# One Trainium2 core, two self attentions: shifts added to the scores by products with ones, and unread products on TensorE

## The chip, the cores and the metric

The kernel runs on one core of one Trainium2 chip. The metric is the device time of one execution in microseconds (us), the median of several runs. The core's engines are TensorE (PE: matmuls, with its weight loads as PEld), VectorE (DVE), ScalarE (ACT), GpSimd (POOL) and SyncE (SP, which here issues DMAs).

## What is computed

A two-layer block on a stream `x` of 32 batches, 64 tokens each, width 128. Each layer has a cross attention over 1601 context rows, a self attention and a feed-forward part. The change is in the two self attentions, one in each layer (16 heads of width 8). Cut to what matters, the first is:

```python
q = _apply_rope((x @ wq).reshape(B, T, H, D), cos, sin)
k = _apply_rope((x @ w_down @ wk_up).reshape(B, T, H, D), cos, sin)
v = (x @ w_down @ wv_up).reshape(B, T, H, D)
scores = jnp.einsum('bqhd,bkhd->bhqk', q, k) / sqrt(D)
scores = jnp.where(allowed, scores, finfo.min)      # pages of 32 tokens
attn = jax.nn.softmax(scores, axis=-1)              # subtracts the row's maximum
out = jnp.einsum('bhqk,bkhd->bqhd', attn, v) @ wo
```

The second has plain projections with biases, and its mask lets a query and a key meet if either is among the 16 most important tokens of its batch.

## The kernel before

The kernel is one program in which each engine follows its own list, and semaphores join them. The stages follow each other: cross attention with the first feed-forward part, self attention SA0, the routed experts, cross attention XA1, self attention SA1, the tree feed-forward part. `self_attention` is called twice, for SA0 and SA1, with the same code. Its order of work is written out by hand, once for each engine.

Work goes in 16 steps, `p` = 0 to 15, of two batches (`u` = 0, 1) each. All 16 heads of both batches go through together. A step has these parts:

- GpSimd (`pool_queries`, L1290) writes the step's queries into `QW`, spread out so that one product serves several heads. For `p` of 4 and more it waits until the scores of step `p - 4` are done.
- TensorE, values (`pe_values`, L1165): one float32 product, two passes in the trace, into a bank of PSUM. VectorE moves it to `VS` with the bias (L1255).
- TensorE, maxima (`pe_maxima`, L1177): 16 products give scores with queries on partitions, two banks. VectorE takes the row maxima (`dve_maxima`, L1263) and writes minus the maximum as two bf16 parts into `MH` (`dve_shift`, L1273 and L1275).
- TensorE, shift products (`pe_shift_rows`, L1190): 16 products turn these columns into rows, two banks, of which two partitions each are used. ScalarE copies three of the four pieces (L1240) and VectorE one (`dve_shift_rows`, L1280) into partitions 32, 33, 96 and 97 of `QW`, next to the queries. The keys `KSA` hold ones there, so the scores come out with the shift in them.
- TensorE, scores (`pe_scores`, L1204): 16 products of 128 columns, with keys on partitions, in four parts of the array (`tile_position`). ScalarE takes the exponential of 128 x 1024 (`act_exp`, L1233).
- TensorE, weighted values (`pe_product`, L1219): 32 float32 products, 64 passes in the trace. ScalarE copies the result to `ABO` (`act_output`, L1245).

In the loop TensorE's order is: scores of `p`, weighted values of `p - 1`, values of `p + 1`, maxima of `p + 3`, shift products of `p + 2`. Ahead of the loop stand values 0, maxima 0 and 1, shift products 0, maxima 2 and shift products 1; I call this and the first steps the opening. The four banks of PSUM from number 4 on go round among values (V), maxima (M) and shift products (R), by the lists `first` and `later`; a job waits until the one four places ahead of it is emptied.

Ahead of SA0 stands the rotary stage (its products L1584 and L1585, VectorE's L1591 to L1600), ahead of SA1 the stage that finds the important tokens. `attention_out` (L1391 and on) follows each.

Of the kernel before, what the change touches and what calls it, by code (L numbers as in the profile page):

```python
# [26 lines left out]
CH = 512  # L27
# [188 lines left out]
def bass_perceiver_kernel(nc, xT, ctxT, wpack, bpack, experts, picks, trees, outT):  # L216
# [3 lines left out]
    with ctx:  # L220
# [37 lines left out]
        MH = sb("MH", [128, 2, 16, 2], BF16)  # L258
        epst = sb("epst", [128, 1], F32)
# [3 lines left out]
        DEC = sb("DEC", [128, 2, CH], BF16)  # L263
# [24 lines left out]


# [822 lines left out]
        def self_attention(role, eng, att, q_stacked, k_stacked, src, banks_ready, between=None):  # L1112


            pairs, kk, rows = B // 2, att.values_k, HALF + 1
            past = 1 if att is SA1 else 0
# [12 lines left out]
            later = [job for p in range(pairs) for job in  # L1129
                     (("V", p + 1, 0), ("M", p + 3, 0), ("M", p + 3, 1), ("R", p + 2, 0), ("R", p + 2, 1))]  # L1130
            for job in first + later:
                if job[1] < pairs:
                    owner.append(job)
                    filled_at[job] = len(owner)
                    by_job = {"act": 2} if job[0] == "R" and job[2] == 0 else emptied_by[job[0]]
# [32 lines left out]
            def pe_maxima(p):  # L1168
                eng.wait_ge(qbuilt, 2 * before + 2 * p + 2)
                if p == pairs // 2:  # L1170
                    eng.wait_ge(*k_stacked[1])
                for h in range(2):
                    bank_free(("M", p, h))
                for u in range(2):
                    for g in range(4):
                        for h in range(2):
                            mm = nc.tensor.matmul(work(("M", p, h))[:, (u * 4 + g) * S:(u * 4 + g + 1) * S],  # L1177
                                                  queries(p, u)[half[h], g * 128:(g + 1) * 128],
                                                  KSA[half[h], g, tokens(p, u)], start=True, stop=True,
                                                  tile_position=(64 * h, 0))  # L1180
                mm.then_inc(filled, 2)

            def pe_shift_rows(p):
                eng.wait_ge(negm, before + p + 1)
                for u in range(2):
                    bank_free(("R", p, u))
                    for g in range(4):
                        for h in range(2):
                            row = 32 + 64 * h
                            mm = nc.tensor.matmul(work(("R", p, u))[row:row + 2, g * 128:(g + 1) * 128],  # L1190
                                                  MH[:, p % 2, h * 8 + u * 4 + g, :], wb("ident16"),
                                                  start=True, stop=True, tile_position=(0, row))
                    mm.then_inc(filled, 1)

            def pe_scores(p):
                for u in range(2):
                    for by in emptied_at[("R", p, u)]:
                        eng.wait_ge(*emptied(("R", p, u), by))
                if before + p:
                    eng.wait_ge(exps, before + p)  # L1200
                for g in range(4):
                    for u in range(2):
                        for h in range(2):
                            mm = nc.tensor.matmul(  # L1204
                                ps[64 * u:64 * u + 64, h, g * 128:(g + 1) * 128], KSA[half[h], g, tokens(p, u)],
                                queries(p, u)[half[h], g * 128:(g + 1) * 128],
                                start=True, stop=True, skip_group_check=True, tile_position=(64 * h, 64 * u))
                mm.then_inc(scores, 1)
# [58 lines left out]
            def dve_shift(p):  # L1267
                for h in range(2):
                    eng.wait_ge(*emptied(("M", p, h), "dve"))
                if p >= 2:  # L1270
                    eng.wait_ge(*filled_with(("R", p - 2, 1)))
# [3 lines left out]
                nc.vector.scalar_tensor_tensor(MH[:, p % 2, :, 1], top, -1.0, MH[:, p % 2, :, 0],  # L1275
                                               ALU.mult, ALU.subtract).then_inc(negm, 1)
# [19 lines left out]
            if role == "pe":  # L1296
                eng.wait_ge(sem("value_pads"), 1)
                eng.wait_ge(*banks_ready)
                pe_values(0)
                eng.wait_ge(sem("ones_set"), 3)  # L1300
# [3 lines left out]
                pe_maxima(1)  # L1304
                pe_shift_rows(0)
# [24 lines left out]
            if role == "dve":  # L1330
                eng.wait_ge(*banks_ready)
                nc.vector.memset(ps[:, 2:4, :].rearrange("p a c -> p (a c)"), 0.0).then_inc(ready, 1)
# [5 lines left out]
                dve_shift_rows(0)  # L1338
                dve_maxima(2)
                dve_shift(2)  # L1340
                dve_shift_rows(1)
                for p in range(pairs):
# [5 lines left out]
                    if p + 2 < pairs:  # L1348
                        dve_shift_rows(p + 2)
# [885 lines left out]
        def program(role, eng):  # L2235
# [8 lines left out]
            if role == "dve":  # L2244
                nc.vector.memset(epst[:, :], EPS).then_inc(sem("eps_set"), 1)
                nc.vector.memset(HM[:, :], 0.0).then_inc(sem("half_zero"), 1)
                nc.vector.memset(VS[:, :, :].rearrange("p u (g i e) -> p (u g) i e", g=8, i=3)[:, :, 1, :], 0.0
# [340 lines left out]
```

## Time and profile before

| what | value |
|---|---|
| median of 3 runs | 1888.97 us (1885.73 to 1890.61) |
| the profiled execution | 1887.62 us, span 1885.8 us |
| TensorE busy | 1739.7 us, 92% of the span, 29724 matmul passes |
| VectorE, ScalarE, GpSimd busy | 1401.4, 1244.4, 581.2 us |
| mean granted TensorE clock | 0.959 |
| SA0 on TensorE | from 653.55 to about 719 us |
| SA1 on TensorE | from 1664.34 to about 1738 us |

The span is the time from the first to the last instruction on the core. Busy is the time in which an engine executes an instruction; TensorE's is modelled from the starts of pipelined matmuls, so starts are more exact than lengths. The granted clock is a share of full speed: 1.0 is 2.4 GHz and 0.5 is 1.2 GHz. The two attentions are about 140 of the 1886 us.

### The profile page before, as it was taken

To read this page: it belongs to the slowest core of one execution; us is meant where nothing else is said; L and a number is where in the kernel's file an instruction comes from. 1 tells how busy PE (TensorE), PEld (TensorE's weight loads), DVE (VectorE), ACT (ScalarE), POOL (GpSimd) and SP (SyncE) were. 2 spreads that over 40 slices of the span, in tenths; PEclk is the share of its full clock that TensorE was granted. 3 is DMA by queue.
4 is the path that set the end of the run, shared out by engine and by line. 5 is a ranking of instruction groups with operands and counts; after the bars stand their busy time and mean duration, and the time that the engine had idled before them with its cause. 6 is when DMAs were issued, how large, how long until landed. Compare 5 with 4: busy or idle time off the path is not lost. (4 is left out here: it accounts for less than half of the span.)

```text
span 1885.8 us, 68279 instructions
## 1 busy us (share of the span) xinstructions
PE 1739.7 (92%) x29724; PEld 1096.8 (58%) x29724; DVE 1401.4 (74%) x2431; ACT 1244.4 (66%) x2177; POOL 581.2 (31%) x463
## 2 busy tenths in 40 slices
PE   7899999999989778799889999999999999866998
PEld 5577777777765456344446666656666665535443
DVE  2577777777752785777789889888988997366565
ACT  3377777777754284224368888888888888367343
POOL 4223222322230350566522232222222220043465
PEclk8799999999999888999989999999999999879999
DMA  4355555555510211465565556555555652030111
GB/s 160 95 133 141 144 145 149 138 143 146 135 31 0 45 27 36 124 157 141 148 110 101 107 97 104 95 107 102 101 102 101 103 100 29 2 71 4 34 40 39
DMA packets 69149, 178.42 MB, mean 95 GB/s; under 512 B 20900, under 2 KB 25124, under 8 KB 68468
## 3 DMA queue, kind: packets, MB, share of 16 engines
q1 hardware_dynamic: 67076, 171.49, 41.4%
q8 instruction: 236, 3.87, 0.9%
q10 hardware_dynamic: 1776, 2.57, 0.7%
q14 instruction: 61, 0.50, 0.1%
HBM read 84.45 MB, written 1.32 MB: 45 GB/s over the span
## 5 line engine op out<-in xcount | busy, mean ns | idle before, releaser
L749 ACT ACTIVATE Pb<-ps 128x512 f32<-128x512 f32 (+1 forms) x832 | 451.9, 597 | 51.4 <-PE ps L693 32.6
L716 PE MATMUL ps<-Pb,V 128*17 128x64 f32 (+1 forms) x13312 | 380.5, 248 | 0.7 <-ACT Pb L749 0.7
L828 DVE TENSOR_REDUCE MX<-ps 128x2 f32<-128x804 f32 (+1 forms) x384 | 363.8, 983 | 21.3 <-PE ps L657 19.9
L716 PEld LDWEIGHTS ps<-Pb,V 128*17 128x17 f32 (+1 forms) x13312 | 250.4, 97 | 87.1 <-issue 43.6
L830 DVE TENSOR_REDUCE MX<-ps 128x1 f32<-128x402 f32 (+1 forms) x512 | 265.9, 569 | 29.8 <-PE ps L661 23.8
L872 POOL TENSOR_TENSOR ABO<-CT 128x1601 bf16<-128x1601 f32 x43 | 123.0, 2863 | 528.6 <-DMA CT<-ctxT 528.6
L752 ACT ACTIVATE Pb<-ps 128x1024 f32<-128x1024 f32 (+1 forms) x224 | 204.6, 959 | 42.6 <-PE ps L697 40.0
L657 PE MATMUL ps<-KST,QW 50*128 50x402 bf16 (+1 forms) x1024 | 176.0, 340 | 13.2 <-DVE C L814 4.5
L693 PE MATMUL ps<-QW,KST 50*128 50x128 bf16 (+1 forms) x3328 | 165.4, 219 | 5.1 <-ACT Pb L749 2.4
L775 ACT ACTIVATE V<-ps 128x512 f32<-128x512 f32 (+1 forms) x256 | 129.5, 521 | 42.4 <-PE ps L597 40.8
L661 PE MATMUL ps<-KST,QW 96*128 96x402 bf16 (+1 forms) x512 | 148.9, 340 | 5.8 <-DVE C L814 0.5
L693 PEld LDWEIGHTS ps<-QW,KST 50*128 50x128 bf16 (+1 forms) x3328 | 104.5, 96 | 73.5 <-ACT Pb L749 44.1
L1779 PE MATMUL ps<-ABO,CT 128*128 128x512 bf16 x362 | 115.2, 384 | 14.0 <-DVE ABO L1841 9.6
L597 PE MATMUL ps<-WS,ABO 128*128 128x128 bf16 x819 | 128.1, 219 | 0.0
L697 PE MATMUL ps<-QW,KST 98*128 98x128 bf16 (+1 forms) x1664 | 124.7, 219 | 2.3 <-ACT Pb L752 1.2
L697 PEld LDWEIGHTS ps<-QW,KST 98*128 98x128 bf16 (+1 forms) x1664 | 108.8, 99 | 16.6 <-ACT Pb L752 1.7
L597 PE MATMUL ps<-WS,CT 128*128 128x128 bf16 (+1 forms) x1118 | 111.2, 220 | 4.3 <-ACT V L775 1.2
L814 DVE SCALAR_TENSOR_TENSOR HL<-ps,W,HL 128x402 bf16<-128x402 f32 x124 | 74.7, 632 | 54.0 <-ACT HL L762 51.5
L814 DVE SCALAR_TENSOR_TENSOR C<-ps,W,C 128x402 bf16<-128x402 f32 (+1 forms) x128 | 77.0, 632 | 44.7 <-ACT C L762 41.8
L1831 ACT ACTIVATE Pb<-ps 128x512 f32<-128x512 f32 x68 | 40.6, 597 | 105.4 <-PE ps L1779 101.1
L657 PEld LDWEIGHTS ps<-KST,QW 50*128 50x128 bf16 x1024 | 51.5, 93 | 87.9 <-issue 43.3
L597 PEld LDWEIGHTS ps<-WS,CT 128*128 128x128 bf16 (+1 forms) x1118 | 87.4, 100 | 24.4 <-issue 12.3
(278 smaller groups left out, 3179.9 us busy)
## 6 DMA issues: line engine op xcount, KB each, us to landing
CT<-ctxT SPq DMA_DIRECT2D x43, 800.5 KB, 4.7
KST<-HL SPq DMA_DIRECT2D x320, 100.1 KB, 3.0
KST<-C SPq DMA_DIRECT2D x320, 100.1 KB, 3.0
Pb<-routed SPq DMA_DIRECT2D x44, 256.0 KB, 4.0
ABO<-ctxT SPq DMA_DIRECT2D x10, 800.5 KB, 5.6
T<-ctxT SPq DMA_DIRECT2D x10, 800.5 KB, 4.4
KST<-HL SPq DMA_DIRECT2D x128, 50.0 KB, 2.7
KST<-C SPq DMA_DIRECT2D x128, 50.0 KB, 2.7
```

The costliest lines, as they stand in the source:

```text
L597: mm = nc.tensor.matmul(work(job)[0:n, i * D:(i + 1) * D], still[:, k0:k0 + n], WS[:, 1, wp, :], start=(k == 0), stop=(k == 2))
L657: mm = nc.tensor.matmul(work(job)[:, h, 0:n], QW[half[h], b % 3, g * 128:(g + 1) * 128], KST[half[h], b % 3, g, c0:c0 + n], start=True, st ...
L661: mm = nc.tensor.matmul(work(job)[:, 0:n], QW[0:RAW, b % 3, g * 128:(g + 1) * 128], KST[0:RAW, b % 3, g, c0:c0 + n], start=True, stop=True)
L693: mm = nc.tensor.matmul(score_bank(b, x, h)[0:n, g * 128:(g + 1) * 128], KST[half[h], b % 3, g, k0:k0 + n], QW[half[h], b % 3, g * 128:(g ...
L697: mm = nc.tensor.matmul(score_bank(b, x, ti)[0:n, g * 128:(g + 1) * 128], KST[0:ROWS, b % 3, g, k0:k0 + n], QW[0:ROWS, b % 3, g * 128:(g + ...
L716: mm = nc.tensor.matmul(ps[32 * quad:32 * quad + m, SUM, oc:oc + nh * S], V[0:n, b % 2, tile, v0:v0 + m], Pb[0:n, buffer(b, x), ti * att.W ...
L749: nc.scalar.activation(Pb[0:n, buffer(b, x), i * 512:(i + 1) * 512], score_bank(b, x, i)[0:n, :], ACT.Exp, scale=att.scale).then_inc(exps, 1)
L752: nc.scalar.activation(Pb[0:n, buffer(b, x), 0:banks * 512].rearrange("p (a c) -> p a c", a=banks), score_banks(b, x)[0:n, 0:banks, :], AC ...
L775: nc.scalar.activation(V[0:n, b % 2, ts[0]:ts[0] + len(ts), 0:att.NV].rearrange("p t (h e) -> p t h e", h=att.H)[:, :, :, 0:att.d], bank[0 ...
L814: nc.vector.scalar_tensor_tensor(keys(b)[:, 1, c0:c0 + n], work(job)[:, 0:n], bias(f"bk{t[-1]}"), keys(b)[:, 0, c0:c0 + n], ALU.add, ALU.s ...
L828: nc.vector.reduce_max(MX[:, b % 2, 2 * j:2 * j + 2], work(job)[:, :, 0:n], AX.X).then_inc(freed["dve"], 1)
L830: nc.vector.reduce_max(MX[:, b % 2, j:j + 1], work(job)[:, 0:n], AX.X).then_inc(freed["dve"], 1)
```

## The change

- The two bf16 parts of the shift go to `MS`, in which 4 groups of 128 columns hold them at columns 0, 1, 32, 33, 64, 65, 96 and 97, the rest zero. 4 shift products turn them into one bank, with every piece on its partitions. ScalarE makes one copy of 128 x 512 into `RW`, which lies in the space of `CL`. VectorE's cast is gone.
- `QW` no longer gets shifts. The scores begin as before, without them, and four products of `ONES` (2 rows, 64 columns) with `RW` (2 rows, 512 columns) add the shift to all scores in PSUM. They wait for ScalarE's copy, where the scores waited before.
- A step has four jobs in the four banks: V, M, M, R.
- `keep_busy(n, bank)` issues `n` products of 128 x 512 in bf16 whose result nothing reads: 12 ahead of SA0, 5 (SA0) or 20 (SA1) behind the first values, 1 ahead of the maxima of each step, 5 ahead of the first shift products.
- Two memsets at the start of VectorE's program, and a wait for them in the attentions. `DEC`, used in the tree stage, now lies in `MS`.

```diff
+        MS = sb("MS", [128, 2, 4, 128], BF16)
+        ONES = sb("ONES", [128, 64], BF16)
...
-        DEC = sb("DEC", [128, 2, CH], BF16)
+        DEC = MS[:, :, :, :].rearrange("p a g c -> p a (g c)")
...
+        def keep_busy(n, bank):
+            for _ in range(n):
+                nc.tensor.matmul(bank, wb("ident16"), WB[:, 0:CH], start=True, stop=True, skip_group_check=True)
...
+            RW = CL[:, 0:2 * 512].rearrange("p (k n) -> p k n", k=2)
...
-            emptied_by = {"V": {"dve": 1}, "M": {"dve": 1}, "R": {"act": 1, "dve": 1}}
-            first = [("V", 0, 0), ("M", 0, 0), ("M", 0, 1), ("M", 1, 0), ("M", 1, 1), ("R", 0, 0), ("R", 0, 1),
-                     ("M", 2, 0), ("M", 2, 1), ("R", 1, 0), ("R", 1, 1)]
+            emptied_by = {"V": {"dve": 1}, "M": {"dve": 1}, "R": {"act": 1}}
+            first = [("V", 0, 0), ("M", 0, 0), ("M", 0, 1), ("M", 1, 0), ("M", 1, 1), ("R", 0, 0),
+                     ("M", 2, 0), ("M", 2, 1), ("R", 1, 0)]
...
                 for h in range(2):
                     bank_free(("M", p, h))
+                keep_busy(1, work(("M", p, 0)))
...
             def pe_shift_rows(p):
                 eng.wait_ge(negm, before + p + 1)
-                for u in range(2):
-                    bank_free(("R", p, u))
-                    for g in range(4):
-                        for h in range(2):
-                            row = 32 + 64 * h
-                            mm = nc.tensor.matmul(work(("R", p, u))[row:row + 2, g * 128:(g + 1) * 128],
-                                                  MH[:, p % 2, h * 8 + u * 4 + g, :], wb("ident16"),
-                                                  start=True, stop=True, tile_position=(0, row))
-                    mm.then_inc(filled, 1)
+                bank_free(("R", p, 0))
+                for g in range(4):
+                    mm = nc.tensor.matmul(work(("R", p, 0))[:, g * 128:(g + 1) * 128], MS[:, p % 2, g, :], wb("ident16"),
+                                          start=True, stop=True)
+                mm.then_inc(filled, 1)
 
             def pe_scores(p):
-                for u in range(2):
-                    for by in emptied_at[("R", p, u)]:
-                        eng.wait_ge(*emptied(("R", p, u), by))
...
-                                start=True, stop=True, skip_group_check=True, tile_position=(64 * h, 64 * u))
+                                start=g == 0, stop=False, skip_group_check=True, tile_position=(64 * h, 64 * u))
+                eng.wait_ge(*emptied(("R", p, 0), "act"))
+                for u in range(2):
+                    for h in range(2):
+                        row = 64 * h + 32 * u
+                        mm = nc.tensor.matmul(ps[64 * u:64 * u + 64, h, :], ONES[row:row + 2, :], RW[row:row + 2, p % 2, :],
+                                              start=False, stop=True, skip_group_check=True, tile_position=(row, 64 * u))
                 mm.then_inc(scores, 1)
...
             def act_shift_rows(p):
-                for u in range(2):
-                    eng.wait_ge(*filled_with(("R", p, u)))
-                    for row in (32, 96) if u == 0 else (32,):
-                        nc.scalar.activation(queries(p, u)[row:row + 2, :], work(("R", p, u))[row:row + 2, :], ACT.Copy
-                                             ).then_inc(freed["act"], 1)
+                eng.wait_ge(*filled_with(("R", p, 0)))
+                nc.scalar.activation(RW[:, p % 2, :], work(("R", p, 0)), ACT.Copy).then_inc(freed["act"], 1)
...
-                top = MX[:, p % 2, 0:16]
-                nc.vector.scalar_tensor_tensor(MH[:, p % 2, :, 0], top, -2.0, top, ALU.mult, ALU.add).then_inc(mx, 1)
+                top = MX[:, p % 2, 0:16].rearrange("p (j g) -> p j g", j=4)
+                hi, lo = [MS[:, p % 2, :, :].rearrange("p g (j r) -> p j g r", j=4)[:, :, :, part]
+                          for part in range(2)]
+                nc.vector.scalar_tensor_tensor(hi, top, -2.0, top, ALU.mult, ALU.add).then_inc(mx, 1)
...
-            def dve_shift_rows(p):
-                eng.wait_ge(*filled_with(("R", p, 1)))
-                nc.vector.tensor_copy(queries(p, 1)[96:98, :], work(("R", p, 1))[96:98, :]).then_inc(freed["dve"], 1)
...
             if role == "pe":
                 eng.wait_ge(sem("value_pads"), 1)
+                eng.wait_ge(sem("shift_pads"), 2)
                 eng.wait_ge(*banks_ready)
                 pe_values(0)
+                keep_busy(20 if past else 5, ps[:, 0, :])
...
                 pe_maxima(1)
+                keep_busy(5, ps[:, 0, :])
                 pe_shift_rows(0)
...
+            if role == "pe":
+                eng.wait_ge(sem("rot_sin"), NC + 1)
+                keep_busy(12, ps[:, 0, :])
             self_attention(role, eng, SA0, q_stacked, k_stacked, C, (sem("rot_rot"), 2 * NC),
```

**TensorE at the opening of SA0.** Before: values, maxima of steps 0 and 1, shift products 0, maxima 2, shift products 1, scores 0.

```order
L1165 MATMUL ps<-W,C 128x144
L1177 MATMUL ps<-KST,QW 128x64 x32
L1190 MATMUL ps<-WB,MH 2x128 x16
L1177 MATMUL ps<-KST,QW 128x64 x16
L1190 MATMUL ps<-WB,MH 2x128 x16
L1204 MATMUL ps<-QW,KST 64x128 x16
```

The same place with the change. L295 is `keep_busy`, L1173 the values, L1186 the maxima, L1196 the shift products, L1206 the scores, L1214 the products with ones.

```order
L295 MATMUL ps<-WB 128x512 x12
L1173 MATMUL ps<-W,C 128x144
L295 MATMUL ps<-WB 128x512 x6
L1186 MATMUL ps<-KST,QW 128x64 x16
L295 MATMUL ps<-WB 128x512
L1186 MATMUL ps<-KST,QW 128x64 x16
L295 MATMUL ps<-WB 128x512 x5
L1196 MATMUL ps<-WB,MS 128x128 x4
L295 MATMUL ps<-WB 128x512
L1186 MATMUL ps<-KST,QW 128x64 x16
L1196 MATMUL ps<-WB,MS 128x128 x4
L1206 MATMUL ps<-QW,KST 64x128 x16
```

25 unread products now stand in the stretch, and each set of shift products is 4 long where it was 16. In SA1 the first 12 are missing and 21 stand in the place of the 6.

**TensorE in one step of the loop.** Before: values and maxima for later steps, shift products, scores, and the weighted values (L1219).

```order
L1165 MATMUL ps<-W,C 128x144
L1177 MATMUL ps<-KST,QW 128x64 x16
L1190 MATMUL ps<-WB,MH 2x128 x16
L1204 MATMUL ps<-QW,KST 64x128 x16
L1219 MATMUL ps<-Pb,VS 18x64 x32
```

With the change (L1227 are the weighted values):

```order
L1173 MATMUL ps<-W,C 128x144
L295 MATMUL ps<-WB 128x512
L1186 MATMUL ps<-KST,QW 128x64 x16
L1196 MATMUL ps<-WB,MS 128x128 x4
L1206 MATMUL ps<-QW,KST 64x128 x16
L1214 MATMUL ps<-CL,ONES 64x512 x4
L1227 MATMUL ps<-Pb,VS 18x64 x32
```

No part changed its place. A step has 81 products before and 74 with the change; the values and the weighted values are float32 and show two passes each in the trace, so 114 and 107 passes.

## Rows read from the trace of the kernel before

**Rows 1.** Windows: us; busy us of PE, PEld, DVE, ACT, POOL; PEclk, DMA, GB/s.
```profile
653.50:673.50 20.00, 14.68 (x360) 11.17 (x360) 18.60 (x31) 11.44 (x20) 14.68 (x14) 0.51 0.40 71
673.50:706.50 33.00, 24.15 (x1030) 18.68 (x1026) 28.80 (x56) 27.76 (x46) 18.97 (x18) 0.95 0.05 10
```

**Rows 2.** PE's timeline at half clock: start us, us, instruction; idle before in brackets.
```profile
669.22 1.01 PE L1190 MATMUL ps<-WB,MH 128*2 128x128 bf16 x16
670.16 0.64 PE L1204 MATMUL ps<-QW,KST 51*64 51x128 bf16 x16
...
673.00 0.61 PE L1190 MATMUL ps<-WB,MH 128*2 128x128 bf16 x16
```

**Rows 3.** PE's timeline at full clock, one step of the second attention.
```profile
1712.67 0.61 PE L1190 MATMUL ps<-WB,MH 128*2 128x128 bf16 x16
1713.21 0.42 PE L1204 MATMUL ps<-QW,KST 51*64 51x128 bf16 x16
1713.56 0.83 PE L1219 MATMUL ps<-Pb,VS 64*18 64x64 f32 x64
1714.32 0.51 PE L1165 MATMUL ps<-W,T 128*128 128x144 f32 x2
1714.77 0.41 PE L1177 MATMUL ps<-KST,QW 51*128 51x64 bf16 x16
```

**Rows 4.** PE's timeline, scores of steps 3, 4 and 13, then 3 and 13.
```profile
673.54 0.43 PE L1204 MATMUL ps<-QW,KST 51*64 51x128 bf16 x16
...
676.78 0.42 PE L1204 MATMUL ps<-QW,KST 51*64 51x128 bf16 x16
...
710.18 0.64 PE L1204 MATMUL ps<-QW,KST 51*64 51x128 bf16 x16
...
1689.52 0.42 PE L1204 MATMUL ps<-QW,KST 51*64 51x128 bf16 x16
...
1727.23 0.42 PE L1204 MATMUL ps<-QW,KST 51*64 51x128 bf16 x16
```

**Rows 5.** PE's timeline, behind stalls of "issue": first and last of each attention.
```profile
677.77 0.76 PE L1219 MATMUL ps<-Pb,VS 64*18 64x64 f32 x56 [0.34 <-issue]
...
706.11 0.49 PE L1190 MATMUL ps<-WB,MH 128*2 128x128 bf16 x11 [0.71 <-issue]
...
1691.05 0.70 PE L1219 MATMUL ps<-Pb,VS 64*18 64x64 f32 x48 [0.86 <-issue]
...
1695.11 0.60 PE L1219 MATMUL ps<-Pb,VS 64*18 64x64 f32 x37 [1.34 <-issue]
...
1728.76 0.81 PE L1219 MATMUL ps<-Pb,VS 64*18 64x64 f32 x62 [0.91 <-issue]
```

**Rows 6.** DMA queues, 673.5 to 706.5 us: queue, packets, MB, share.
```profile
q8 instruction: 8, 0.13, 1.8%
```

**Rows 7.** Groups by line, 673.5 to 706.5 us: xcount; busy us, mean ns; idle.
```profile
L1240 ACT ACTIVATE QW<-ps 2x512 bf16<-2x512 f32 x28 | 16.5, 589 | 5.4 <-PE ps L1190 4.6
...
L1280 DVE CAST QW<-ps 2x512 bf16<-2x512 f32 x9 | 6.3, 697 | 0.3
```

**Rows 8.** PE's timeline in the tree stage, full clock, 512 columns in bf16.
```profile
1769.91 0.39 PE L1974 MATMUL ps<-T,CT 128*128 128x512 bf16 x1
1770.14 0.39 PE L1974 MATMUL ps<-T,ABO 128*128 128x512 bf16 x1
```

**Rows 9.** Timelines of the two openings: PE, DVE, then PE in the second.
```profile
653.55 0.82 PE L1165 MATMUL ps<-W,C 64*128 64x144 f32 x2 [6.12 <-DVE ABO L1597]
...
655.94 1.27 DVE L1263 TENSOR_REDUCE MX<-ps 128x8 f32<-128x512 f32 x2
...
1671.64 0.61 PE L1177 MATMUL ps<-KST,QW 51*128 51x64 bf16 x16 [6.82 <-POOL QW L1290]
...
1674.94 1.02 PE L1190 MATMUL ps<-WB,MH 128*2 128x128 bf16 x16 [0.54 <-DVE MH L1275]
```

**Rows 10.** DVE's timeline, its first work behind the opening memsets.
```profile
10.59 1.74 DVE L814 SCALAR_TENSOR_TENSOR HL<-ps,W,HL 128x402 bf16<-128x402 f32 x3 [9.52 <-ACT HL L762]
```

More of the change, by code:

```diff
@@ L1125, in self_attention @@
             owner, filled_at, emptied_at, count = [], {}, {}, {"act": 0, "dve": 0}
-            emptied_by = {"V": {"dve": 1}, "M": {"dve": 1}, "R": {"act": 1, "dve": 1}}
-            first = [("V", 0, 0), ("M", 0, 0), ("M", 0, 1), ("M", 1, 0), ("M", 1, 1), ("R", 0, 0), ("R", 0, 1),
-                     ("M", 2, 0), ("M", 2, 1), ("R", 1, 0), ("R", 1, 1)]
+            emptied_by = {"V": {"dve": 1}, "M": {"dve": 1}, "R": {"act": 1}}
+            first = [("V", 0, 0), ("M", 0, 0), ("M", 0, 1), ("M", 1, 0), ("M", 1, 1), ("R", 0, 0),
+                     ("M", 2, 0), ("M", 2, 1), ("R", 1, 0)]
             later = [job for p in range(pairs) for job in
-                     (("V", p + 1, 0), ("M", p + 3, 0), ("M", p + 3, 1), ("R", p + 2, 0), ("R", p + 2, 1))]
+                     (("V", p + 1, 0), ("M", p + 3, 0), ("M", p + 3, 1), ("R", p + 2, 0))]
             for job in first + later:
@@ L1134, in self_attention @@
                     filled_at[job] = len(owner)
-                    by_job = {"act": 2} if job[0] == "R" and job[2] == 0 else emptied_by[job[0]]
+                    by_job = emptied_by[job[0]]
                     for by, n in by_job.items():
@@ L1203, in pe_scores @@
                         for h in range(2):
-                            mm = nc.tensor.matmul(
+                            nc.tensor.matmul(
                                 ps[64 * u:64 * u + 64, h, g * 128:(g + 1) * 128], KSA[half[h], g, tokens(p, u)],
                                 queries(p, u)[half[h], g * 128:(g + 1) * 128],
-                                start=True, stop=True, skip_group_check=True, tile_position=(64 * h, 64 * u))
+                                start=g == 0, stop=False, skip_group_check=True, tile_position=(64 * h, 64 * u))
[5 more added lines that the diff above has]
+                                              start=False, stop=True, skip_group_check=True, tile_position=(row, 64 * u))
                 mm.then_inc(scores, 1)
@@ L1270, in dve_shift @@
                 if p >= 2:
-                    eng.wait_ge(*filled_with(("R", p - 2, 1)))
-                top = MX[:, p % 2, 0:16]
-                nc.vector.scalar_tensor_tensor(MH[:, p % 2, :, 0], top, -2.0, top, ALU.mult, ALU.add).then_inc(mx, 1)
-                eng.wait_ge(mx, before + p + 1)
-                nc.vector.scalar_tensor_tensor(MH[:, p % 2, :, 1], top, -1.0, MH[:, p % 2, :, 0],
-                                               ALU.mult, ALU.subtract).then_inc(negm, 1)
-            def dve_shift_rows(p):
-                eng.wait_ge(*filled_with(("R", p, 1)))
-                nc.vector.tensor_copy(queries(p, 1)[96:98, :], work(("R", p, 1))[96:98, :]).then_inc(freed["dve"], 1)
+                    eng.wait_ge(*filled_with(("R", p - 2, 0)))
+                top = MX[:, p % 2, 0:16].rearrange("p (j g) -> p j g", j=4)
+                hi, lo = [MS[:, p % 2, :, :].rearrange("p g (j r) -> p j g r", j=4)[:, :, :, part]
+                          for part in range(2)]
+                nc.vector.scalar_tensor_tensor(hi, top, -2.0, top, ALU.mult, ALU.add).then_inc(mx, 1)
+                eng.wait_ge(mx, before + p + 1)
+                nc.vector.scalar_tensor_tensor(lo, top, -1.0, hi, ALU.mult, ALU.subtract).then_inc(negm, 1)
             def pool_queries(p):
@@ L1331, in self_attention @@
                 eng.wait_ge(*banks_ready)
+                eng.wait_ge(sem("shift_pads"), 2)
                 nc.vector.memset(ps[:, 2:4, :].rearrange("p a c -> p (a c)"), 0.0).then_inc(ready, 1)
@@ L1337, in self_attention @@
                 dve_shift(1)
-                dve_shift_rows(0)
                 dve_maxima(2)
                 dve_shift(2)
-                dve_shift_rows(1)
                 for p in range(pairs):
@@ L1347, in self_attention @@
                         dve_shift(p + 3)
-                    if p + 2 < pairs:
-                        dve_shift_rows(p + 2)
             if role == "pool":
@@ L2246, in program @@
                 nc.vector.memset(HM[:, :], 0.0).then_inc(sem("half_zero"), 1)
+                nc.vector.memset(MS[:, :, :, :].rearrange("p a g c -> p (a g c)"), 0.0).then_inc(sem("shift_pads"), 1)
+                nc.vector.memset(ONES[:, :], 1.0).then_inc(sem("shift_pads"), 1)
                 nc.vector.memset(VS[:, :, :].rearrange("p u (g i e) -> p (u g) i e", g=8, i=3)[:, :, 1, :], 0.0
```

## Prediction

> **What bounds the kernel now.** I began with the table of windows, to see which engine fills the two self attentions. In the first 20 us of the first one, the opening, TensorE has a mean granted clock of 0.51, which is the 1.2 GHz level nearly throughout. In the 33 us behind it the clock is 0.95, the 2.4 GHz level for all but a few microseconds, and TensorE is busy 24.15 us, VectorE 28.80 and ScalarE 27.76 [rows 1]. None is full, so the bound is not one engine's busy time. I then read TensorE's timeline for the length of one step (a pair of batches). At half clock the shift products of one step and of the next start 3.78 us apart with no gap inside: there TensorE is the bound [rows 2]. At full clock the pieces of a step take 0.54 for the 16 shift products, 0.35 for the 16 scores, 0.76 for the 64 passes of the weighted values and 0.45 for the values; with the maxima's 0.41 this is 2.5 us of work [rows 3]. But the steps are not 2.5 us long. Scores of step 3 to scores of step 13 are 36.64 us apart in the first attention and 37.71 in the second, so 3.66 and 3.77 us for one step [rows 4].
>
> What fills the other 1.2 us is in the next view: idle time that ends in "issue", so with no engine waited for. Ten such stalls stand in the second attention between 1691.05 and 1728.76, nine distances of 4.19 us; in the first one the stalls from 677.77 to 706.11 bound seven distances of 4.05 us, of which one has no visible stall at its end [rows 5]. They are not tied to a place of the program: 48 of a step's 64 value passes are left behind the first, 37 behind the second [rows 5]. So one comes after 114 + 11 = 125 matmul passes. The queue that carries instructions moved 8 packets, 0.13 MB, in the 33 us, which is one of some 16 KB for each distance [rows 6]. I read this as TensorE's instruction supply: one packet holds what 125 passes and their weight loads need, and packets come 4.05 to 4.19 us apart when TensorE wants them faster. Check: 114 / 125 x 4.05 = 3.69 and 114 / 125 x 4.19 = 3.82, against 3.66 and 3.77 measured.
>
> The Trainium skill, page "Runtime: NRT & Kernel Launch", section "Instruction fetch mechanics", says that instructions come in 16 KiB blocks of 256 and that crossing a block's end is mostly hidden. The size agrees with the packets; "mostly hidden" does not agree with stalls of 0.86 and 0.91 us. By that rule the supply would set nothing and the shorter instruction list would give nothing, which is the first rival below.
>
> **The change, part by part.** (1) Shift products: 16 become 4. Scores: 4 products with ones are added. One unread product is added per step. The step has 114 - 12 + 4 + 1 = 107 passes. If the supply sets the pace, it falls in that ratio: 3.66 x 7/114 = 0.22 and 3.77 x 7/114 = 0.23 us a step. Ten steps in each attention run so: -2.2 and -2.3, together **-4.5 us**. Steps 13 to 15 have fewer shift products or none but keep their ones, and I count nothing there.
>
> (2) What TensorE itself does in a step. Of 512 columns in bf16 the nearest rows start 0.23 us apart [rows 8]; 4 new shift products have 512 columns in all, so 0.23 for 0.54. The unread product: 0.23. The four products with ones have 512 columns each, in four different parts of the array. The trace has none like them. If they run one after another they take 0.92; if all four run together, 0.23. The nearest row is the scores: 16 products of 128 columns, also 2048 in all and also in four parts, take 0.35 [rows 3]. I take 0.35 and keep both ends. The step becomes 2.51 - 0.54 + 0.23 + 0.23 + 0.35 = 2.78 us, below the supply's 3.44 to 3.54, so at full clock it costs nothing. At half clock it costs: 3.78 - 0.94 + 0.43 + 0.43 + 0.64 = 4.34 us, 0.6 more than now (0.43 is 512 columns at 1.2 GHz, 0.64 the scores at half clock, for the ones, 0.94 the shift products [rows 2]). So the change needs the clock to be up.
>
> (3) ScalarE and VectorE lose work: three copies of 0.589 become one of the same columns, -1.18 us a step; VectorE's cast of 0.697 goes [rows 7]. In the steady part both hide behind the supply, worth nothing more. In the openings VectorE is the one that is full (18.60 of 20.00 us [rows 1]) and a cast stands between one step's shift and the next step's maximum; three casts lie on the way to the scores of step 3: -0.7 x 3 = -2.1 in each opening.
>
> (4) Unread products in the openings. First attention: 12 while TensorE sits idle (6.12 us idle before 653.55 [rows 9]); they cost nothing since they last 2.8 us by rows 8. Then 5 and 1 ahead of the first maximum. If the clock has fallen by 653.55 as now, they take 6 x 0.43 = 2.6 us. Now VectorE begins that maximum at 655.94, and the products are ready about 655.0 (653.55 + 0.82, and 0.61 for 16 maxima [rows 9]), so 1.0 of it is covered: +1.6. Five more stand before the shift products, which wait for VectorE anyhow; covered. In return TensorE works without a gap from 653.55 on, and the clock rises with it: three steps fall from 3.78 to 3.5, -0.8. Sum of this opening: 1.6 - 2.1 - 0.8 = **-1.3 us**. Second attention: 20 fill the 6.82 us before the first maximum at 1671.64, which waits for GpSimd and not for them (20 x 0.23 = 4.6 us). Then one before each maximum and 5 before the shift products, which start at 1674.94 now [rows 9]: by up to 5 x 0.43 = 2.1 us later at half clock, by 0.7 at full clock since they begin about 1674.4. I take the middle, +1.4. Sum: 1.4 - 2.1 - 0.8 = **-1.5 us**.
>
> (5) Two memsets at the start of VectorE lie in its idle 9.52 us before its first product [rows 10]; without that cover they would cost about 1 us, by the 1.27 us of two reduces over 512 columns [rows 9]. The new waits on them, and TensorE's wait for the rotary stage, are long over where they stand: by the timeline TensorE is idle there. The wait for ScalarE's copy moves behind the scores and has a step's time.
>
> Sum: -4.5 - 1.3 - 1.5 = -7.3. The profiled execution took 1887.62 us (span 1885.8), so 1880.3. It lay 1.35 below the median of the runs, so the median should be **1881.7 us**, 0.4% faster. A measurement of this kernel tells 0.3%, 5.7 us, from no change.
>
> **Rivals.** (A) The block's end costs nothing in itself, and the gaps have another cause, such as one wait per step: then the 7 passes are worth nothing and only the openings gain, 1888.97 - 2.8 = 1886. For it: one of eight block ends at full clock in the first attention shows no stall, and a step there took 3.24 us, from 673.54 to 676.78 [rows 4]. Against it: the stalls wander by 11 passes a step. (B) Taking work from ScalarE and VectorE lets the pace fall to the 3.24 us of that step: (3.66 - 3.24 + 3.77 - 3.24) x 10 = -9.5, with the openings -12.3: 1877. For it: ScalarE needs three copies in each step and was 84% busy [rows 1, 7]. Against: it would have to outrun the 4.05 us. (C) Slower: the four products with ones run one after another and meet a half clock in the openings. Then a step is 3.78 - 0.94 + 0.43 + 0.43 + 4 x 0.43 = 5.42 us, +1.64 in six steps, +9.8; the starts come 1.6 and 2.1 late; nothing is saved by the casts, as TensorE is the bound; the steady part still gains 4.5 (0.92 in place of 0.35 gives 3.35 us, under the pace). 9.8 + 3.7 - 4.5 = +9: 1898. It decides once a step at half clock exceeds about 4.9 us and the clock stays there for three steps. Against it: scores already overlap in four parts.
>
> The Trainium skill, page "TensorEngine Tiling (Array Packing)", section "Key Properties", says that changing the tiling mode drains TensorE, and each step gets one change more, from the scores' parts to the smaller parts of the ones. The trace shows no price for one; it would push toward (C) at half clock and hide under the pace at full clock.
>
> **How the numbers follow.** The forecast 50%, and its own range is 1876 to 1887; A 20%; B 16%; C 9%; 5% for what I don't see, such as block ends that shift in other stages. Range: A, B and the forecast with its bounds reach from 1874 to 1889, C is left out. Faster by over 0.3% (below 1883.3): 0.8 of the forecast's 0.50 and B's 0.16, 0.56. Slower: C and a part of the rest, 0.11. Within: 0.33.
>
> **What would show it.** Scores of step 3 to step 13 in 34.4 and 35.4 us; stalls of "issue" still there, some 4.1 us apart, and moving by 125 - 107 = 18 passes a step. Clock up before the scores of step 1 in both openings. Products with ones: 0.35 from first start to next work. Three-copy waits of ScalarE gone. The forecast is wrong if the steps keep 3.66 and 3.77 us (A), if the stalls thin out and a step takes 3.24 (B), or if TensorE's clock stays at half past the third scores while steps exceed 4.9 us (C).

## The result and the profile after

The changed kernel is **slower**: 1901.97 us median (1892.44 to 1912.38, 17 runs) against 1888.93 (1883.02 to 1894.85, 17 runs), ratio 1.007 [1.0055, 1.0084]. The forecast was 1881.7. The profiled execution of the changed kernel took 1892.44 us (span 1890.6) and was the fastest of its runs, so the two traces are only 4.8 us apart and show a part of the 13 us. Its clock was also the highest: the mean granted clock of the 17 runs of the changed kernel lies from 0.942 to 0.954 (median 0.950), so the typical run spent more time at half clock than this trace shows.

| profiled execution | before | after |
|---|---|---|
| TensorE busy, passes | 1739.7 us, 29724 | 1773.1 us, 29547 |
| VectorE, ScalarE busy | 1401.4, 1244.4 us | 1386.7, 1207.3 us |
| mean granted TensorE clock | 0.959 | 0.954 |
| SA0: first value product to last weighted value | 65.3 us | 79.5 us |
| the same for SA1 | 73.2 us | 68.7 us |

The two attentions answer for +14.2 - 4.5 = +9.7 us. Outside them the changed kernel was 4.9 us shorter in this execution (1742.4 against 1747.3 us of span). Only the two memsets and the 12 unread products ahead of SA0 were added there. In the traces of the later kernels that part took 1743 to 1755 us, without an order in it, so the 4.9 us are no effect of the change that could be shown.

The windows, for [rows 1]: the opening of SA0, its other steps, then the steady part of SA1 (us; busy us of PE, PEld, DVE, ACT, POOL; PEclk, DMA, GB/s).

```profile
648.40:663.00 14.60, 12.34 (x130) 5.73 (x130) 12.26 (x18) 3.37 (x6) 11.40 (x11) 0.62 0.48 85
663.00:719.90 56.90, 56.90 (x1356) 34.71 (x1352) 25.39 (x63) 24.91 (x38) 23.17 (x22) 0.50 0.06 11
...
1701.90:1733.30 31.40, 25.64 (x965) 16.90 (x963) 30.27 (x46) 17.06 (x27) 18.69 (x18) 1.00 0.07 14
```

The second row is the loss. For 56.9 us TensorE is busy all the time, and the granted clock is 0.50 throughout, the 1.2 GHz level. Before, it was 0.95 in the 33 us behind the opening. The third row shows something else: full clock, TensorE with a gap in every step, and VectorE busy 30.27 of 31.40 us.

TensorE's timeline in SA0: the first values, for [rows 9]; scores 0 and the next wait; the scores of step 3; one step at half clock, for [rows 2]; the scores of step 13 (start us, us, instruction; L295 is the unread product, L1214 the ones):

```profile
648.42 0.82 PE L1173 MATMUL ps<-W,C 64*128 64x144 f32 x2 [3.47 <-DVE ABO L1599]
...
658.77 0.42 PE L1206 MATMUL ps<-QW,KST 51*64 51x128 bf16 x16
...
661.92 0.61 PE L1196 MATMUL ps<-WB,MS 128*128 128x128 bf16 x4 [1.29 <-DVE MS L1282]
...
671.67 0.64 PE L1206 MATMUL ps<-QW,KST 51*64 51x128 bf16 x14
...
676.28 0.64 PE L1206 MATMUL ps<-QW,KST 51*64 51x128 bf16 x16
676.85 0.64 PE L1214 MATMUL ps<-CL,ONES 2*64 2x512 bf16 x4
677.42 1.14 PE L1227 MATMUL ps<-Pb,VS 64*18 64x64 f32 x64
678.49 0.84 PE L1173 MATMUL ps<-W,C 64*128 64x144 f32 x2
679.27 0.61 PE L295 MATMUL ps<-WB 128*128 128x512 bf16 x1
679.81 0.61 PE L1186 MATMUL ps<-KST,QW 51*128 51x64 bf16 x16
680.35 0.61 PE L1196 MATMUL ps<-WB,MS 128*128 128x128 bf16 x4
680.89 0.64 PE L1206 MATMUL ps<-QW,KST 51*64 51x128 bf16 x16
...
717.74 0.64 PE L1206 MATMUL ps<-QW,KST 51*64 51x128 bf16 x16
```

The scores of step 0 take 0.42 us, as at full clock, so the clock did rise in the opening. Behind TensorE's wait of 1.29 us for VectorE the pieces take half-clock times, and they keep them to the end of SA0. The step is 680.89 - 676.28 = 4.61 us, without a gap: scores 0.57, ones 0.57, weighted values 1.07, values 0.78, unread 0.54, maxima 0.54, shift products 0.54. From step 3 to step 13 it is 46.07 us, where [rows 4] have 36.64.

One step of SA1 at full clock, the engines together (idle before in brackets), for [rows 3]; ahead of it and behind it the scores of steps 3 and 13:

```profile
1701.95 0.49 PE L1206 MATMUL ps<-QW,KST 51*64 51x128 bf16 x16
...
1711.04 1.08 DVE L1282 SCALAR_TENSOR_TENSOR MS<-MX,MS 128x16 bf16<-128x16 f32 x1
1712.18 0.40 PE L1196 MATMUL ps<-WB,MS 128*128 128x128 bf16 x4 [0.63 <-DVE MS L1282]
1712.51 0.42 PE L1206 MATMUL ps<-QW,KST 51*64 51x128 bf16 x16
1712.85 0.41 PE L1214 MATMUL ps<-CL,ONES 2*64 2x512 bf16 x4
1713.19 0.83 PE L1227 MATMUL ps<-Pb,VS 64*18 64x64 f32 x64
1713.36 2.16 POOL L1292 TENSOR_TENSOR QW<-QS,HM 115x512 bf16<-115x512 bf16 x2 [1.32 <-PE ps L1214]
1713.58 0.90 DVE L1280 SCALAR_TENSOR_TENSOR MS<-MX 128x16 bf16<-128x16 f32 x1
1714.52 1.08 DVE L1282 SCALAR_TENSOR_TENSOR MS<-MX,MS 128x16 bf16<-128x16 f32 x1
1715.66 0.40 PE L1196 MATMUL ps<-WB,MS 128*128 128x128 bf16 x4 [0.63 <-DVE MS L1282]
...
1736.15 0.42 PE L1206 MATMUL ps<-QW,KST 51*64 51x128 bf16 x16
```

The stalls of "issue" of [rows 5] are gone from TensorE's matmul rows; in their place TensorE waits 0.63 us for VectorE's second shift instruction. The step is 1715.66 - 1712.18 = 3.48 us and repeats to 0.01. It is a closed chain: shift products, scores and ones take 1.18 us until GpSimd, which waited for the ones, starts its two query instructions; these last 2.16; VectorE's shift ends 0.08 behind them; 0.06 later the shift products start. VectorE's two small instructions (128x16) take 0.90 and 1.08 us there. When GpSimd is idle they take 0.23 each (DVE's timeline, opening of SA1):

```profile
1689.40 0.23 DVE L1280 SCALAR_TENSOR_TENSOR MS<-MX 128x16 bf16<-128x16 f32 x1
1689.67 0.23 DVE L1282 SCALAR_TENSOR_TENSOR MS<-MX,MS 128x16 bf16<-128x16 f32 x1
```

### The profile page after: what moved, and what is told of

It reads as the page before. It is cut to its first block and busy times, and to the rows that moved or that the text cites. A ratio compares the mean times of both kernels' runs of the same rounds, so it can differ in the third digit from the quotient of the medians.

```text
span 1890.6 us, 67766 instructions
## 1 busy us (share of the span) xinstructions
PE 1773.1 (94%) x29547; PEld 1100.6 (58%) x29547; DVE 1386.7 (73%) x2401; ACT 1207.3 (64%) x2113; POOL 579.5 (31%) x463
## 3 DMA queue, kind: packets, MB, share of 16 engines
HBM read 84.45 MB, written 1.32 MB: 45 GB/s over the span
## 5 line engine op out<-in xcount | busy, mean ns | idle before, releaser
L835 DVE TENSOR_REDUCE MX<-ps 128x2 f32<-128x804 f32 (+1 forms) x384 | 364.3, 986 | 21.4 <-PE ps L664 19.8
```

The source lines that it names most:

```text
L835: nc.vector.reduce_max(MX[:, b % 2, 2 * j:2 * j + 2], work(job)[:, :, 0:n], AX.X).then_inc(freed["dve"], 1)
```

## The experiments

Each kernel was timed beside the kernel before. "Attentions" is the length of SA0 and SA1 in the profiled execution, from the first value product to the last weighted value. The last column is the sum of the two less that of before (138.5 us), beside ratio - 1 times 1888 us.

| kernel | median us (runs) | ratio [95%] | attentions us | difference: trace, times |
|---|---|---|---|---|
| the change | 1901.97 (17) | 1.0070 [1.0055, 1.0084] | 79.5, 68.7 | +9.7, +13.2 |
| e1 change, no unread products | 1888.88 (12) | 1.0003 [0.9985, 1.0021] | 69.8, 69.4 | +0.7, +0.6 |
| e2 before, with unread products | 1892.18 (12) | 1.0024 [1.0007, 1.0041] | 70.5, 72.3 | +4.3, +4.5 |
| e8 change, ones of 16 rows | 1899.18 (12) | 1.0053 [1.0032, 1.0073] | 78.2, 67.0 | +6.7, +10.0 |
| e3 change, ones of 32 rows | 1882.28 (12) | 0.9977 [0.9959, 0.9994] | 63.1, 69.0 | -6.4, -4.3 |
| e4 ones of 64 rows | 1880.93 (12) | 0.9970 [0.9951, 0.9989] | 61.8, 67.2 | -9.5, -5.7 |
| e5 e4, first shift part from one input | 1883.39 (12) | 0.9981 [0.9967, 0.9996] | 66.1, 68.5 | -3.9, -3.6 |
| e7 e4, none unread per step | 1878.29 (7) | 0.9953 [0.9935, 0.9972] | 60.8, 67.0 | -10.7, -8.9 |
| e6 e4, no unread products | 1873.63 (6) | 0.9922 [0.9901, 0.9942] | 59.4, 65.8 | -13.3, -14.7 |
| e9 e6, first shift part by ScalarE | 1869.16 (6) | 0.9899 [0.9881, 0.9918] | 57.7, 64.9 | -15.9, -19.1 |
| e10 e6, one shift part only | 1868.63 (6) | 0.9898 [0.9872, 0.9923] | 56.3, 63.7 | -18.5, -19.3 |

### The two halves of the change apart (e1, e2)

e1 takes the unread products out of the change; e2 adds them, and nothing else, to the kernel before.

```diff
 def keep_busy(n, bank):
-    for _ in range(n):
+    for _ in range(0):
```

> The changed kernel without any unread product; everything else stays. Theory 1 (the new form of the shift keeps the half clock: four products of which each uses 2 rows of the array): the first attention still runs most of its steps at a clock of 0.5, now 4.61 - 0.54 = 4.07 us each, and the time stays above before, near 1895 us. Theory 2 (the unread product of each step is what lengthens a half-clock step and holds it there): the clock comes back within the first steps, steps take about 3.5 us, and the time is 1880 to 1888 us.

> The kernel before with all unread products and its old form of the shift. Theory 1: the clock comes back as in the kernel before, the openings are better or the same, a full-clock step has 115 passes and is paced by instructions, so the time is within 4 us of before. Theory 2: the first attention stays at half clock with steps of 3.78 + 0.54 = 4.3 us and the time is 10 us or more above before.

In e1 and e2 the windows of SA0 read so (e1 the first row):

```profile
663.00:720.00 57.00, 56.46 (x1561) 39.13 (x1565) 26.59 (x66) 29.30 (x44) 23.66 (x23) 0.50 0.08 15
```

```profile
663.00:706.00 43.00, 32.61 (x1277) 22.71 (x1272) 34.76 (x71) 35.81 (x58) 25.09 (x24) 1.00 0.12 22
706.30:716.50 10.20, 9.60 (x243) 6.46 (x242) 5.31 (x12) 5.58 (x10) 0.00 (x0) 0.50 0.02 3
```

The unread products are not what holds the clock down: in e1 it is also 0.50 from 650.7 us, the start of SA0, to 720. (Its expectation had the mechanism right and the size wrong: 1888.88 us and not 1895, since the step is 3.95 us and not 4.07.) They make the half clock dear: e1's step there is 3.95 us, the change's 4.61, and 0.66 a step is 6.6 us in ten steps. In the old code (e2) most of SA0 is at full clock, as it was without them. There they raise the clock earlier: in the first 20 us of SA0 it is 0.77 on average, where [rows 1] have 0.51. But they buy no time with it, as e2 is 4.2 us slower than before. So something in the new products keeps the clock down.

### How many rows the products with ones use (e3, e8, e4)

The new products read 2 rows of the array's 128. In e3 they read 32, in e8 16; the added rows of `RW` are zero, so instructions, durations and result are the same.

```diff
-ONES[row:row + 2, :], RW[row:row + 2, p % 2, :]
+ONES[row:row + 32, :], RW[row:row + 32, p % 2, :]
```

> The changed kernel with 32 rows in each product with ones in place of 2 (the other 30 rows of the copy are zero, so the result is the same). No time of an instruction should change. Theory 1 in its form 'few rows of the array at work keep the clock down': the clock comes back in the first attention, steps of 3.5 us, time below 1890 us. If the rows don't matter (the form of the shift costs only by its length, or by its change of tiling): as the changed kernel, 4.61 us a step in most of the first attention and a median near 1902 us.

> The changed kernel with 16 rows in each product with ones, between the changed kernel's 2 and e3's 32 (the added rows are zero). If the rows at work decide by degree: some executions with the first attention at half clock, median between 1882 and 1902, near 1888. If it is a matter of few against many: like e3 (1882) or like the changed kernel (1902).

e3, the whole of SA0 behind its first 9 us, and a step in it:

```profile
657.10:711.20 54.10, 45.16 (x1673) 29.58 (x1671) 45.19 (x72) 30.16 (x47) 26.44 (x26) 1.00 0.12 22
```

```profile
682.12 0.40 PE L1196 MATMUL ps<-WB,MS 128*128 128x128 bf16 x4 [0.53 <-DVE MS L1282]
682.45 0.42 PE L1206 MATMUL ps<-QW,KST 51*64 51x128 bf16 x16
682.79 0.41 PE L1214 MATMUL ps<-CL,ONES 32*64 32x512 bf16 x4
683.13 0.83 PE L1227 MATMUL ps<-Pb,VS 64*18 64x64 f32 x64
```

e8:

```profile
663.00:719.30 56.30, 55.79 (x1288) 34.02 (x1288) 25.52 (x63) 23.91 (x36) 23.52 (x23) 0.50 0.08 15
...
682.48 0.64 PE L1206 MATMUL ps<-QW,KST 51*64 51x128 bf16 x16
683.05 0.64 PE L1214 MATMUL ps<-CL,ONES 16*64 16x512 bf16 x4
```

With 32 rows the clock is 1.00, the ones take 0.34 us as they do with 2 rows at full clock, and the kernel is 20 us faster than the change by medians. The granted clocks of all runs say the same as the two traces: 0.962 to 0.972 in e3's twelve, 0.942 to 0.954 in the change's 17.

e3's trace alone does not show a clock that comes back. It rose in the opening, at about 657 us, and at the same wait for VectorE where the change lost it, it stayed up:

```profile
661.20 0.40 PE L1196 MATMUL ps<-WB,MS 128*128 128x128 bf16 x4 [1.22 <-DVE MS L1282]
```

With 16 rows nothing comes back in the trace, and eleven of the twelve runs took 1892.78 us or more. One took 1884.07, at a mean granted clock of 0.969, like e3's runs. It has no trace, but its clock says that with 16 rows the loop does not stay at half clock in every execution.

In e4 the ones use 64 rows, in the same four parts of the array as the scores (the matrix of ones holds zeros except in two rows for each batch):

```diff
-row = 64 * h + 32 * u
-... ONES[row:row + 2, :], RW[row:row + 2, p % 2, :]
+row = 64 * h
+... ONES[row:row + 64, u, :], RW[row:row + 64, p % 2, :]
```

> The changed kernel with the products with ones in the same four parts of the array as the scores (64 rows, ones in 2 of them, zero in the rest), so without the change of tiling between scores and ones and between a 32-row part and what follows. If the change of tiling is what costs: the products with ones take less than 0.57 us at half clock (0.43 to 0.46), a half-clock step 4.5 us or less, and the clock comes back in the first attention. If not: 4.61 us and a median near 1902 us. If only the rows count, as e3.

```profile
681.99 0.42 PE L1206 MATMUL ps<-QW,KST 51*64 51x128 bf16 x16
682.24 0.39 PE L1214 MATMUL ps<-CL,ONES 64*64 64x512 bf16 x4
682.56 0.83 PE L1227 MATMUL ps<-Pb,VS 64*18 64x64 f32 x64
```

Scores and ones together take 0.57 us where e3's take 0.68, and the step falls from 3.48 to 3.36. By times e3 and e4 can't be told apart (the intervals overlap); by steps they can. e4 changes the parts of the array and the number of rows together, so which of the two gives the 0.11 us is not shown.

### What paces a step at full clock (e5, e7, e6)

First theory: VectorE's shift stands still beside GpSimd because it reads two operands from SBUF.

```diff
-nc.vector.scalar_tensor_tensor(hi, top, -2.0, top, ALU.mult, ALU.add)
+nc.vector.tensor_scalar(hi, top, -1.0, None, ALU.mult)
```

> e4 with the first part of the shift computed from one operand (maximum times -1, the same value) in place of two. In e4 a full-clock step is 3.36 us long and VectorE has no gap: 0.29 + 1.27 + 0.78 + 1.08, with both parts of the shift (0.78 and 1.08) while GpSimd writes queries. Theory V (VectorE is the bound at full clock because an instruction with two operands in SBUF waits for GpSimd's): the first part falls to about 0.2, the step to 3.36 - 0.6 = 2.8 us or to what comes next, and if my theory of the instruction supply holds, stalls of 'issue' come back with 107 passes a step and 125 a packet, so a step is not under about 3.3 us and the gain is 0 to 2 us in all. Rival (the supply doesn't bound): steps of 2.8 us and 10 us less in all, near 1872 us.

```profile
680.08 2.16 POOL L1292 TENSOR_TENSOR QW<-QS,HM 115x512 bf16<-115x512 bf16 x2 [1.20 <-PE ps L1214]
680.42 0.75 DVE L1280 TENSOR_SCALAR MS<-MX 128x16 bf16<-128x16 f32 x1
681.21 1.11 DVE L1282 SCALAR_TENSOR_TENSOR MS<-MX,MS 128x16 bf16<-128x16 f32 x1
```

That theory fell: with one input the instruction also takes 0.75 us (0.78 in e4), ends with GpSimd's first one, and the step stays at 3.36. e5's attentions are 5.6 us longer than e4's in the traces, but outside the steady steps: 1.9 in SA0's opening, and a step of 5.02 and one of 3.93 us ahead of the scores of step 13. By times the two can't be told apart. The unread products were then taken out of e4, first those of each step (e7), then all (e6).

> e4 without the one unread product of each step, the ones in the openings kept. At full clock VectorE sets the step, so 3.36 us as in e4; at half clock a step is 0.54 us shorter than in e4. If the product of each step matters for the clock, this shows dips inside the attentions that e4 doesn't have; otherwise the median is within 2 us of e4, 1879 to 1883 us.

> e4 without any unread product. If the clock comes back by the form of the products with ones alone: full-clock steps of 3.36 us as in e4, the clock up by the fourth step in both attentions, median within 3 us of e4 (1881). If the unread products are needed for the clock: long stretches at half clock with steps of about 3.95 us, median near 1888 us as e1.

e6 gains 7.3 us on e4 by medians. e7's 2.6 lie within overlapping intervals. The gain is not in the step, which is 3.36 us in all three. Taking TensorE's 0.33 us out of a step only lengthens its wait for VectorE (e6, 1680 to 1710 us, where it is 6.1 us in 8 steps; and the window named below):

```profile
PE ps L1196 <- DVE MS L1282: 6.1, 8, 0.9
```

```profile
660.00:667.00 7.00, 5.29 (x136) 3.57 (x132) 5.79 (x11) 2.90 (x4) 4.42 (x5) 0.50 0.46 81
```

What the traces show of the gain is in the openings: from the first value product to the scores of step 3, e4 takes 19.8 and 25.7 us, e6 18.4 and 23.7, although e6's clock was still at half from 660 to 667 us, in SA0's opening. That is 3.4 of the 3.8 us between the two traces' attentions; the rest of the 7.3 is not in these traces.

e6 and e1 are also the plainest pair for the clock. Neither has unread products, and both reach the scores of step 0 at half clock, 9.31 and 9.30 us behind the first values. e1, with 2 rows, stays at half clock to the end of SA0. In e6, with 64 rows, the clock comes back between steps 1 and 2 (e6, its products with ones in these steps):

```profile
665.63 0.64 PE L1214 MATMUL ps<-CL,ONES 64*64 64x512 bf16 x4
...
668.49 0.39 PE L1214 MATMUL ps<-CL,ONES 64*64 64x512 bf16 x4
```

Against the change, then, 1901.97 - 1873.63 = 28 us come from 64 rows and no unread products.

### The chain against the instruction supply (e9, e10)

e9 lets ScalarE write the first part of the shift, a pair ahead, so that VectorE has one small instruction left (`act_shift` for `p + 2` is called ahead of `act_exp(p)`); e10 leaves the second part out of the computation.

```diff
+            def act_shift(p):
+                nc.scalar.activation(hi, top, ACT.Copy, scale=-1.0).then_inc(mx, 1)
...
-                nc.vector.scalar_tensor_tensor(hi, top, -2.0, top, ALU.mult, ALU.add).then_inc(mx, 1)
```

> From the kernel with 64 rows and no unread products (1873.63 us, steps of 3.36 us at full clock, of which TensorE waits 0.85 us for VectorE's second shift instruction). Here ScalarE writes the first bf16 part of the shift, a pair ahead, and VectorE only the second. Chain theory (a step lasts as long as: shift products, scores, products with ones, GpSimd's two query instructions, VectorE's shift, which stands still while GpSimd's run): one shift instruction of VectorE's is left, of 0.2 us when alone; it fits ahead of GpSimd's instructions or between them, the wait of 0.85 us goes, and the step falls to 2.6 to 3.1 us; ten steps of full clock per attention give 5 to 14 us in all, so 1860 to 1868 us. Rival, the supply of TensorE's instructions: the step cannot fall under about 3.3 us for 106 passes (one packet of 125 passes in some 4 us); waits named issue come back inside the products and the time stays within 3 us of 1873.6. Second rival, the place in GpSimd's queue: VectorE's remaining instruction still ends 0.08 us after GpSimd's queries, the step stays at 3.36 us exactly, without waits named issue.

> From the same kernel. The second bf16 part of the shift is left out of the computation (the shift is rounded to its first bf16 part), so VectorE has one shift instruction of 0.2 us when alone and ScalarE has no more than before. Chain theory: as with the shift split between two engines, the wait of 0.85 us goes or shrinks to what GpSimd's instruction still holds VectorE for, the step falls to 2.6 to 3.1 us, 1860 to 1868 us in all. Supply rival: step not under 3.3 us, waits named issue return. If this kernel gains and the one with ScalarE's instruction does not, ScalarE's place in the chain (an instruction put ahead of its exponential) is the cause; if neither does, the one instruction left still waits out GpSimd's and the step stays at 3.36 us.

e9, five of the eight TensorE rows with idle time of "issue" in the steady part of SA1, and two scores among them:

```profile
1680.41 0.20 PE L1186 MATMUL ps<-KST,QW 51*128 51x64 bf16 x2 [0.79 <-issue]
...
1684.74 0.24 PE L1206 MATMUL ps<-QW,KST 51*64 51x128 bf16 x2 [1.01 <-issue]
...
1687.00 0.42 PE L1206 MATMUL ps<-QW,KST 51*64 51x128 bf16 x16
...
1688.53 0.72 PE L1227 MATMUL ps<-Pb,VS 64*18 64x64 f32 x51 [0.64 <-issue]
...
1690.29 0.42 PE L1206 MATMUL ps<-QW,KST 51*64 51x128 bf16 x16
...
1691.99 0.44 PE L1227 MATMUL ps<-Pb,VS 64*18 64x64 f32 x30 [0.60 <-issue]
...
1708.06 0.76 PE L1227 MATMUL ps<-Pb,VS 64*18 64x64 f32 x56 [0.57 <-issue]
```

Each theory held for a part. The wait for VectorE is gone and single steps are now as short as 2.33 us, so the chain did set the 3.36. But the old stalls are back at once: seven distances from 1680.41 to 1708.06, 3.95 us each on average, and from 1688.53 to 1691.99 there are 51 + 42 + 34 = 127 passes. The mean step is 3.07 us in SA0 and 3.24 in SA1 (scores 3 to 13 in 30.7 and 32.4 us), with steps from 2.3 to 3.9. e10 is the same with less work (3.15 and 3.21 us), so ScalarE's extra instruction costs nothing that shows. e9 computes everything and is the fastest such kernel here: 1.0% faster than before, 1.7% than the change by medians.

## Why the prediction was wrong, point by point

**The step that failed** is in (4): "In return TensorE works without a gap from 653.55 on, and the clock rises with it." The clock did rise, before the scores of step 0, but it fell again at TensorE's next wait; from then on TensorE worked without a gap for 56.9 us, and the clock stayed at half. That is shown by the window above, and e3 shows what it hangs on: 32 rows in place of 2, with all else equal, and the clock is up. Work without a gap was not enough. The text had said that "the change needs the clock to be up" and priced the half clock at +0.6 a step, but for the opening alone. Over SA0's ten steps, 4.61 - 3.66 = 0.95 us each is +9.5 where (1) had -2.2. The Trainium skill, page "TensorE: Matmul & The Clock Gate", section "What's actually happening", ties the clock to how busy TensorE has been; this trace, busy 56.90 of 56.90 us at 1.2 GHz, does not agree if "busy" means the time in matmuls.

**(1) The supply, -4.5 us.** The reading of the kernel before holds: when e9 and e10 removed the chain, stalls came back every 125 to 127 passes, on average 3.7 to 4.0 us apart. But in the changed kernel the supply paces neither attention. SA1's steps fell to 3.42 us on average (34.20 us from 1701.95 to 1736.15, forecast 35.4), and the agreement is chance: VectorE and GpSimd set 3.48. "In the steady part both hide behind the supply" missed that one chain through three engines, none of them full by its own work, can be longer than the supply's time. Steps 13 to 15 with their end, at which the prediction counted nothing, cost 1.5 us in SA0, at half clock, and gave 2.4 in SA1.

**(2) TensorE's own pieces.** The ones took 0.34 us at full clock (taken: 0.35) and 0.57 at half (0.64). The half-clock step was 4.61 against 4.34, since a piece that was priced at 0.43 started the next one 0.54 later (unread and shift products), and since the values and maxima, which take 1.21 us together in e1, take 1.32 when an unread product stands between them.

**(3) and (4), the openings.** From the first value product to the scores of step 3, SA0 took 23.25 us against 19.99 (forecast -1.3, measured +3.3) and SA1 26.56 against 25.18 (forecast -1.5, measured +1.4). That the unread products delay the first maximum was right: VectorE began it 4.08 us after the first values, 1.7 later than in [rows 9] (2.39), forecast +1.6:

```profile
652.50 1.29 DVE L1268 TENSOR_REDUCE MX<-ps 128x8 f32<-128x512 f32 x2 [1.72 <-PE ps L1186]
```

Without the unread products the openings are 1.4 and 2.0 us shorter (e6 against e4). The casts were priced too high at -2.1 in each opening: without unread products the forecast's terms give -2.1 - 0.8 = -2.9, and e6, whose clock comes back, is 1.5 us below before in each. Up to the scores of step 0 their loss gave nothing: 9.30 us in e1 and 9.31 in e6, where before had 9.15. VectorE fills the place of the 0.70 us cast with its second shift instruction, which meets GpSimd's there (1.08 us in e6, from 660.78; 0.18 before, from 661.13).

**The rivals.** C was nearest in time (1898), by its second condition alone: the clock stayed down, but for the whole of SA0, with steps of 4.61 and not over 4.9, and with four products with ones that overlapped. A and B are not what happened; a step near B's 3.24 came only with e9 and e10. **(5)** The memsets: VectorE's first instruction behind them starts at 10.60 where [rows 10] have 10.59, nothing, as said.

What stays open: why few rows hold the clock down at all, and why SA1, with the same products, gets its clock back while SA0 does not. In the change's SA1 the clock fell at about 1695 us and was up again at 1702; in e8's it was 0.50 only from 1694.6 to 1700.4, in the opening, and 1.00 in the loop; e1's came back as well. One difference is visible: SA0's values are read from 64 rows, SA1's from 128 (`64*128` and `128*128` in the rows of L1173). It wasn't tried. Each kernel has one trace; the times and granted clocks of all runs speak for the same order. The attentions of the two traces leave 3 of the 13 us unexplained. The lower clocks of the change's other runs fit more half clock in them, but none of them has a trace.

## What to carry to other kernels

Where a change adds matmuls that read few of the array's rows, price the stretch at both clock levels, and try them padded with zeros to 32 or 64 rows: here the padding cost nothing and moved the time by 20 us, though only one of the two loops with these products had lost its clock for good. Products that nothing reads are no substitute; they cost 4 us in the old kernel and 7 in the best form of the new one. And once one pacing resource is relieved, look for the closed chain through the other engines: a step that repeats to 0.01 us while TensorE waits in each is a sign of one.

## What the runs showed that was not expected

- In SA0's loop a TensorE busy without a gap stays at 1.2 GHz for 57 us when each step contains four products of 2 rows and 512 columns, and in the trace with 16 rows too; with 32 or 64 rows it is at 2.4 GHz. In SA1's loop the same 2-row products held the clock at half for about 7 us at most in the traces.
- VectorE's 128x16 instructions take 0.23 us beside an idle GpSimd and 0.75 to 1.11, with one input or two, beside its tensor_tensor of 115x512; they end within 0.1 us of GpSimd's. The kernel before has this too: 0.96 us for L1275 at 657.89, while GpSimd writes queries from 657.78 on. The Trainium skill, page "SBUF — State Buffer", section "SBUF: two separate sides", calls the port pair that the two share an exclusive lock, which for VectorE takes a fast mode or two inputs from SBUF. For the two-input form the trace agrees, 1.08 us; for the one-input form, 0.75, it doesn't show which mode the instruction ran in.
- Scores and ones together take 0.57 us at full clock when the ones use the scores' parts of the array and 64 rows (e4), and 0.68 in parts of their own with 32 rows (e3).
